# Two attention layers: TensorE's slots in pairs, sums in 32-column tiles, denominators inverted through transposes

## What is computed

```python
def layer0(x, ...):                       # x: (2, 512, 48, 48), 8 heads of 64, n = 2304 tokens
    xn = group_norm(x); qkv = qkv_w @ xn + qkv_b
    w = softmax(q . k / 8)                # per image and head: 2304 x 2304
    return proj_w @ (w . v) + proj_b + x
def layer1(h, ...):                       # queries and keys also see a position embedding
    q, k, v = [h, emb] @ Wq, [h, emb] @ Wk, h @ Wv
    return softmax(q . k / 8) . v @ Wout + bout + h
```

## Time and profile before

| | us |
|---|---|
| median of 3 runs | 4704.73 (4703.88 to 4705.93) |
| the profiled execution, its own time | 4705.96 |
| its span, first to last instruction | 4703.8 |
| granted clock of TensorE, mean | 0.993 |

### The profile page before, as it was taken

The page is one execution under the profiler, slowest core; times in us unless marked ns, Lnnn a source line. Parts: engine busy times, 40 slices in busy tenths (PEclk is TensorE's granted clock), DMA queues, the critical chain, the costliest instruction groups (busy, mean ns, idle before and its releaser), DMA issues. The chain is left out here.

```text
span 4703.8 us, 77022 instructions
## 1 busy us (share of the span) xinstructions
PE 4551.0 (97%) x25368; PEld 2453.8 (52%) x25368; DVE 3318.6 (71%) x3948; ACT 2820.0 (60%) x2981; POOL 2314.1 (49%) x1160
## 2 busy tenths in 40 slices
PE   7997999999999999998999979999999999999989
PEld 4554555555555555554555545555555555555545
DVE  4224888888888888888433358888888888888872
ACT  1113777777777777776001137777777777777750
POOL 0001666666666666666100026666666666666650
PEclk9999999999999999999999999999999999999999
DMA  4334121211111111110444431111111111111206
GB/s 192 131 124 118 25 61 28 54 35 45 42 45 45 37 45 35 48 43 32 167 146 149 147 104 31 50 38 42 46 41 45 37 47 34 50 37 45 59 20 214
DMA packets 234728, 321.66 MB, mean 68 GB/s; under 512 B 12080, under 2 KB 221104, under 8 KB 233648
## 3 DMA queue, kind: packets, MB, share of 16 engines
q1 hardware_dynamic: 214512, 292.61, 21.3%
q10 hardware_dynamic: 20160, 28.32, 1.6%
HBM read 188.76 MB, written 132.12 MB: 68 GB/s over the span
## 5 line engine op out<-in xcount | busy, mean ns | idle before, releaser
L618 POOL TENSOR_TENSOR prob<-prob,mx 128x768 f32<-128x768 f32 x1152 | 2293.1, 2025 | 2227.6 <-ACT mx L763 2227.6
L756 ACT ACTIVATE prob<-psum_att 128x1152 f32<-128x1152 f32 x1152 | 1302.3, 1130 | 587.1 <-DVE run L851 510.5
L700 PE MATMUL psum_att<-qst,kst 128*128 128x384 f32 x6912 | 1513.4, 354 | 44.6 <-DMA kst<-qk_scratch 27.4
L769 ACT ACTIVATE prob<-prob 128x1152 f32<-128x1152 f32 x1152 | 1340.8, 1164 | 356.2 <-DVE prob L618 355.2
L700 PEld LDWEIGHTS psum_att<-qst,kst 128*128 128x128 f32 x6912 | 1156.5, 189 | 452.3 <-issue 427.1
L713 PE MATMUL psum_att<-prob,vst 128*64 128x384 f32 x6912 | 1348.3, 502 | 15.4 <-ACT prob L769 9.2
L851 DVE TENSOR_TENSOR run<-psum_att,run 128x1152 f32<-128x1152 f32 x768 | 1039.1, 1353 | 370.1 <-PE psum_att L700 359.8
L618 DVE TENSOR_TENSOR prob<-prob,mx 128x384 f32<-128x384 f32 x1152 | 1015.5, 882 | 1.7 <-ACT mx L763 1.7
L713 PEld LDWEIGHTS psum_att<-prob,vst 128*64 128x64 f32 x6912 | 405.4, 136 | 532.1 <-issue 491.0
L721 PE MATMUL psum_att<-prob,const_sb 128*32 128x384 f32 x6912 | 677.1, 494 | 0.0
L321 PE MATMUL psum<-xc_l,wq 128*128 128x384 f32 x1536 | 504.1, 489 | 10.8 <-DVE hl_l L426 5.6
(11 more groups left out here) (53 smaller groups left out, 1633.6 us busy)
## 6 DMA issues: line engine op xcount, KB each, us to landing
qk_scratch<-hl_l SPq DMA_DIRECT2D x48, 1536.0 KB, 5.6
qst<-qk_scratch SPq DMA_DIRECT2D x192, 384.0 KB, 5.4
kst<-qk_scratch SPq DMA_DIRECT2D x192, 192.0 KB, 3.3
v_scratch<-vo_l SPq DMA_DIRECT2D x24, 768.0 KB, 3.5
vst<-v_scratch SPq DMA_DIRECT2D x96, 192.0 KB, 2.5
att_scratch<-ob ACTq DMA_DIRECT2D x96, 192.0 KB, 1.9
attc_l<-att_scratch SPq DMA_DIRECT2D x24, 768.0 KB, 6.0
x_sb<-in_x SPq DMA_DIRECT2D x8, 1152.0 KB, 14.3
```

The costliest lines, as they stand in the source:

```text
L618: return engine.tensor_tensor(x[:, :, q0:q1], x[:, :, q0:q1], m, ALU.subtract)
L700: mm = nc.tensor.matmul(psum[:, 3 * (s % 2) + k, 0:CH], kst[:, e, (3 * c + k) * P:(3 * c + k + 1) * P], qst[par][:, 2 * w + e, :], start=( ...
L756: nc.scalar.activation(chunk_of(par, s), s_bank(s), ACT.Copy).then_inc(copied, 1)
L769: nc.scalar.activation(x, x, ACT.Exp, scale=SCALE).then_inc(exp_done, 1)
```

## The change

TensorE's body goes by chunks: the scores of slots 2c and 2c + 1, then one `weigh` with three key tiles and one or two pairs of denominators, six times a block. The v sums are split into 32-column tiles as well, two for each head, so that all sums have one tile shape. The denominators are transposed in slot 8 (`turn_den`), added, inverted and widened by three small DVE operations on 3 x 2 numbers for each partition, transposed back in slot 10 (`spread_den`), and `norm` reads them in PSUM, in the same block, in place of block and slot t + 3, 3. The copies of both sums stand side by side at slot 6 of ACT, ahead of that slot's exp; the copy `dsp` and the six long reciprocals go. `SHIFT_DVE` stays 128 of 384.

```diff
@@ -29,17 +29,16 @@
 GN_EPS = 1e-5
 NORM_STEPS = 10
 SHIFT_DVE = 128
+POOL_BEHIND = False
 SHIFT_LAG = 15
 EXP_LAG = 16
 PV_LAG = 18
-PV_TILES = [[0, 1], [2], [3, 4], [5], [6, 7], [8], [9, 10], [11], [12, 13], [14], [15, 16, 17], []]
-DEN_PAIRS = [[], [0], [], [1, 2], [], [3], [], [4, 5], [], [6], [], [7, 8]]
-PV_END = 10
-FREE_AT = [3, 3, 7, 7, 11, 11]
-REDUCE_AT, BROADCAST_AT, SPREAD_AT = 0, 2, 8
-INVERT_AT = [9, 12, 12, 13, 13, 14]
-PARTS = len(INVERT_AT)
-NORM_AT, STORE_AT = 3, 4
+PV_COLS = 32
+DEN_PAIRS = [[0], [1, 2], [3], [4, 5], [6], [7, 8]]
+FREE_AT = [1, 1, 3, 3, 5, 5]
+TURN_AT, BROADCAST_AT = 0, 2
+EVACUATE_AT, DEN_TURN_AT, DEN_SPREAD_AT = 6, 8, 10
+STORE_AT = 0
 
 
 def is_block(t, *numbers):
@@ -648,7 +648,7 @@
                         for c in range(KC):
-                            sp.wait_ge(pv_done, pv_count(t - 2, 2 * c + 1))
+                            sp.wait_ge(pv_done, pv_count(t - 2, c))
                             sp.dma_start(
@@ -661,15 +661,17 @@
-            pe.sem_inc(pv_done, 2 * SLOTS)
+            pe.sem_inc(pv_done, 2 * KC)
...
             def bank_free(t, s):
...
-                if not before(t, 2) and s == SPREAD_AT + 2 and live(t - 2):
-                    pe.wait_ge(spread_copied, t - 1)
+                if not before(t, 2) and s == DEN_TURN_AT + 2 and live(t - 2):
+                    pe.wait_ge(den_summed, t - 1)
+                if not before(t, 3) and s == DEN_SPREAD_AT + 2 - SLOTS and live(t - 3):
+                    pe.wait_ge(normed, t - 2)
@@ -683,10 +685,16 @@
-            def spread_den(t, s):
+            def turn_den(t, s):
                 pe.wait_ge(den_copied, t + 1)
                 for r in range(3):
-                    mm = nc.tensor.matmul(spare_bank(s, r), sel, den[:, r * P:(r + 1) * P], start=True, stop=True)
+                    mm = nc.tensor.transpose(spare_bank(s, r), den[:, r * P:(r + 1) * P], ident)
+                mm.then_inc(den_turned, 1)
+
+            def spread_den(t, s):
+                pe.wait_ge(widened, t + 1)
+                for r in range(3):
+                    mm = nc.tensor.transpose(spare_bank(s, r), dwide[:, r, :], ident)
                 mm.then_inc(spread, 1)
@@ -702,17 +710,18 @@
                                               qst[par][:, 2 * w + e, :], start=(w == 0), stop=(w == 1))
                 mm.then_inc(scored, 1)
 
-            def weigh(t, par, v):
-                if v == 0 and not before(t, 1):
+            def weigh(t, par, c):
+                if c == 0 and not before(t, 1):
                     pe.wait_ge(pv_copied, t)
-                for kt in PV_TILES[v]:
-                    if kt % 3 == 0:
-                        pe.wait_ge(v_in[kt // 3], 16 * (t // JB + 1))
-                        pe.wait_ge(exp_done, SLOTS * t + 2 * (kt // 3) + 2)
+                pe.wait_ge(v_in[c], 16 * (t // JB + 1))
+                pe.wait_ge(exp_done, SLOTS * t + 2 * c + 2)
+                for kt in range(3 * c, 3 * c + 3):
                     for e in range(2):
-                        mm = nc.tensor.matmul(psum[e * D:(e + 1) * D, 6, 0:CH], vst[:, kt, e * D:(e + 1) * D],
-                                              prob[par][:, e, kt, :], start=(kt == 0), stop=(kt == KT - 1))
-                for j in DEN_PAIRS[v]:
+                        for d in range(e * D, (e + 1) * D, PV_COLS):
+                            mm = nc.tensor.matmul(psum[d:d + PV_COLS, 6, 0:CH], vst[:, kt, d:d + PV_COLS],
+                                                  prob[par][:, e, kt, :], start=(kt == 0), stop=(kt == KT - 1),
+                                                  tile_position=(0, d))
+                for j in DEN_PAIRS[c]:
                     if j == 0 and not before(t, 1):
                         pe.wait_ge(den_copied, t)
                     for e in range(2):
@@ -724,20 +733,24 @@
             def body(t, par):
-                for s in range(SLOTS):
-                    bank_free(t, s)
-                    if not before(t, 1) and live(t - 1):
-                        if s in (REDUCE_AT, REDUCE_AT + 1):
-                            turn(t - 1, s, s - REDUCE_AT)
-                        if s in (BROADCAST_AT, BROADCAST_AT + 1):
-                            broadcast_max(t - 1, s, s - BROADCAST_AT)
-                    if not before(t, 2) and live(t - 2) and s == SPREAD_AT:
-                        spread_den(t - 2, s)
-                    if live(t):
-                        scores(t, par, s)
-                    tv, pv, v = behind(t, par, s, PV_LAG)
+                for c in range(KC):
+                    for s in (2 * c, 2 * c + 1):
+                        bank_free(t, s)
+                        if not before(t, 1) and live(t - 1):
+                            if s in (TURN_AT, TURN_AT + 1):
+                                turn(t - 1, s, s - TURN_AT)
+                            if s in (BROADCAST_AT, BROADCAST_AT + 1):
+                                broadcast_max(t - 1, s, s - BROADCAST_AT)
+                        if not before(t, 2) and live(t - 2):
+                            if s == DEN_TURN_AT:
+                                turn_den(t - 2, s)
+                            if s == DEN_SPREAD_AT:
+                                spread_den(t - 2, s)
+                        if live(t):
+                            scores(t, par, s)
+                    tv, pv, sv = behind(t, par, 2 * c, PV_LAG)
                     if live(tv):
-                        weigh(tv, pv, v)
+                        weigh(tv, pv, sv // 2)
@@ -768,23 +781,13 @@
-            def copy_weighted(t, par):
-                act.wait_ge(pv_done, pv_count(t, PV_END))
-                if not before(t, 2):
-                    act.wait_ge(normed, t - 1)
-                nc.scalar.activation(pvr[par][:, :], pv_bank, ACT.Copy).then_inc(pv_copied, 1)
-
-            def copy_den(t):
-                act.wait_ge(pv_done, pv_count(t, SLOTS - 1))
+            def copy_weighted(t):
+                act.wait_ge(pv_done, pv_count(t, KC - 1))
                 if not before(t, 1):
-                    act.wait_ge(spread, t)
+                    act.wait_ge(normed, t)
+                    act.wait_ge(den_turned, t)
+                nc.scalar.activation(pvr[:, :], pv_bank, ACT.Copy).then_inc(pv_copied, 1)
                 nc.scalar.activation(den[:, :], den_bank, ACT.Copy).then_inc(den_copied, 1)
-
-            def copy_spread(t, s):
-                act.wait_ge(spread, t + 1)
-                if not before(t, 1):
-                    act.wait_ge(inverted, PARTS * t)
-                nc.scalar.activation(three(dsp[:, :]), spare(s), ACT.Copy).then_inc(spread_copied, 1)
@@ -795,19 +798,15 @@
             def body(t, par):
                 for s in range(SLOTS):
+                    if s == EVACUATE_AT and not before(t, 2) and live(t - 2):
+                        copy_weighted(t - 2)
                     te, pe_, se = behind(t, par, s, EXP_LAG)
                     if live(te):
                         exponential(te, pe_, se)
-                    if s == 5 and not before(t, 2) and live(t - 2):
-                        copy_weighted(t - 2, par)
-                    if s == 6 and not before(t, 2) and live(t - 2):
-                        copy_den(t - 2)
                     if live(t):
                         copy(t, par, s)
                     if s in (BROADCAST_AT, BROADCAST_AT + 1) and not before(t, 1) and live(t - 1):
                         copy_max(t - 1, 1 - par, s, s - BROADCAST_AT)
-                    if s == SPREAD_AT and not before(t, 2) and live(t - 2):
-                        copy_spread(t - 2, s)
                     if s == STORE_AT and not before(t, 3) and live(t - 3):
                         store(t - 3, 1 - par)
@@ -824,6 +823,8 @@
                         pool.wait_ge(copied, SLOTS * t + s + 1)
+                        if POOL_BEHIND:
+                            pool.wait_ge(dve_shifted, SLOTS * t + s + 1)
                         shift_part(nc.gpsimd, par, s, SHIFT_DVE, CH).then_inc(pool_shifted, 1)
@@ -863,36 +864,47 @@
                 dve.wait_ge(copied, SLOTS * t + s + 1)
                 shift_part(nc.vector, par, s, 0, SHIFT_DVE).then_inc(dve_shifted, 1)
 
-            def invert(t, part):
-                dve.wait_ge(spread_copied, t + 1)
+            def invert(t, s):
+                dve.wait_ge(den_turned, t + 1)
+                if live(t + 2):
+                    dve.wait_ge(scored, scored_count(SLOTS * (t + 2) + s))
                 if not before(t, 1):
-                    dve.wait_ge(normed, t)
-                q = slice(part * CH // PARTS, (part + 1) * CH // PARTS)
-                nc.vector.reciprocal(rec[:, q], dsp[:, q]).then_inc(inverted, 1)
-
-            def norm(t, par):
-                dve.wait_ge(inverted, PARTS * (t + 1))
+                    dve.wait_ge(inverted, t)
+                groups = spare(s).rearrange("p r (e o i) -> p r e o i", e=2, o=2)[:, :, :, :, 0]
```

(66 more changed lines are left out.)

## The result

The changed kernel took 4763.3 us (median of 4 runs, 4761.2 to 4763.9) against 4705.3 for the kernel before on the same chip: 1.0122 times as long, 95% interval 1.0105 to 1.014. The profiled execution's span is 4761.4 us. The forecast was 4750, range 4640 to 4840.

A forecast was written before the change was run, and what follows sets the result against it. POOL's loop through DVE's folds was to bound the changed kernel: 34.24 + 3.39 = 37.63 us, with 0.1 for the copy 37.7 a block. 92 x (37.7 - 37.17) = +49, less 4, gave 4750 us, range 4640 to 4840.

The forecast's parts named there:

- The loop through POOL: T1, POOL's second subtraction 12.23 us later, 11 subtractions, DVE's last folds, next T1: 37.63 us after the change.
- T1: TensorE's transpose of the second head's folded maximum, marking a block; forecast starts 37.4 to 38.0 us apart.
- TensorE's own work: TensorE's block after the change: 34.3 us, 2.9 less than 37.17, through fewer changes of form.
- Waits at the turns: TensorE waits for DVE's folds at both turns, 3.3 us a block, since POOL's loop ends later.
- 36.98 us, 0.19 short of the period: POOL's loop in the kernel before, 11.58 + 22.01 + 3.34 + 0.05, against a period of 37.17 us.
- T0: TensorE's transpose of the first head's folded maximum, one slot before T1; forecast to have 2 us to give.
- 0.65 + 0.1 - 0.19 = 0.56: Block's growth: POOL's loop 0.65 us longer, 0.1 for the widening copy, less 0.19 slack; forecast block 37.7 against 37.17.
- the port free at the folds: Rival: POOL done, or DVE let in twice, before DVE's folds; T1 at 35.1, 4508 us; chance near 4508: 0.06.
- The widening copy: Small DVE copy for denominators; taking its turn makes POOL's stretch 0.33 us longer; 0.1 added for that.
- The plain reading: Rival: TensorE alone bounds the kernel, its 2.9 us a block kept whole, 4434 us; chance of whole gain 0.03.

The follow-up runs named there:

- two runs: Kernel before with the subtraction shared 160 to 224, 4654.4 us; kernel before with POOL all but taken away, 4643.4 us; both 36.68 us a block.
- the kernel with the places moved: Changed kernel with subtraction shared 160 to 224, denominators' pairs dealt out anew, and their two transposes one slot earlier (slots 7 and 9): 4632.0 us.
- two of them, with POOL relieved: Kernel before with 32-column v tiles, subtraction shared 160 to 224, and three pairs of slots running their scores back to back: 4529.3 us.

## Why the prediction was right, and where not

- **The loop through POOL** was right in kind and size: second subtraction 12.23 us after T1, forecast 12.23; 11 subtractions in 22.17, forecast 22.01 and 0.1 more; POOL's end to T1 3.45, forecast 3.39. Moving the pairs out of the loop, with no less work, gave 89 us.
- **TensorE's own work**: `weigh` with two pairs 3.37, as forecast; 32-column tiles cost what 64-column ones do, and the change of form 0.14 (3.51 with wide tiles). Waits at the turns are 3.04 us, forecast 3.3.
- **"36.98 us, 0.19 short of the period" was wrong.** I closed POOL's loop only through DVE's folds to T1. It closes earlier, in slot 0. POOL's end is at 1032.99, the first head's fold ends behind it, and T0 starts at 1033.46; TensorE's undisturbed slot 0 takes 2.97 from T0 to T1, which makes 3.44. The path that ends last goes on from that fold through DVE's subtraction, ACT's exp and slot 0's v sums to T1 at 1036.58, 3.59 after POOL's end. With 11.58 and 22.01 this is 37.18, the whole period. The kernel before was bound by POOL's loop, not by TensorE, whose order takes 36.68 (two runs). The difference of period was therefore 0.65 + 0.16 - 0.13 = 0.68, where I had 0.65 + 0.1 - 0.19 = 0.56 and rounded to 0.53; the missing 0.15 us a block are 14 us, about what the forecast was low by.
- **"T1 at 35.1" for the port free at the folds**: 35.60 with POOL almost gone. The missing term is slot 5's wait for the second maximum's copy: 0.56 us, 2.86 against 2.3 for slots 4 and 5.
- **The widening copy** takes turns with POOL, 0.68 us in place of 0.36. POOL's stretch grew by 0.16 us, of which 0.12 lie in the subtraction beside the copy. I had given the copy 0.1, between nothing and a turn of 0.33; that it came out so near was luck, not a reading. In the kernel with the places moved the same copy waited a whole us longer, a term that my expectation there put at nothing.
- **The plain reading** (TensorE's 2.9 us kept whole) had no part in it. Undoing the narrow tiles cost a sixth of what it would have cost had TensorE set the end.

## What to carry to other kernels

An engine that is busy 97% of the span need not be the bound: add up every loop from one event back to itself, through each place where it can close, and compare with the period. When an engine gets faster, look where its instructions' places move within the slower loop: here a longer `weigh` between two events of POOL's loop cost more than 2.4 us less work on TensorE brought. Take the parts of such a change one by one: two of them, with POOL relieved, gave 3.8%.

## What the runs showed of the hardware

TensorE keeps its clock over the two idle pieces of the changed kernel (1.65 and 1.39 us, granted clock 1.00 in the block). With the fold as a reduction the idle time lies in one piece of 2.66 us ahead of T1. The clock then fell in 18 of some 92 blocks (0.92 to 0.96 in the mean of such a block), and their periods were 38.5 to 40.3 us in place of 37.41; in the others the same wait of about 2.66 us left it at 0.99 to 1.00. TensorE in order of time in one of the 18, and the clock (the seventh column) right behind the wait and in a usual block:

```profile
1119.09 0.90 PE L679 MATMUL psum_att<-const_sb,fold 128*128 128x128 f32 x3 [2.66 <-DVE fold L857]
1119.65 2.27 PE L708 MATMUL psum_att<-qst,kst 128*128 128x384 f32 x6
1121.85 3.78 PE L721 MATMUL psum_att<-prob,vst 128*32 128x384 f32 x24
```

```profile
1118.40:1125.20 6.80, 6.11 (x33) 3.46 (x37) 3.06 (x6) 5.55 (x6) 0.00 (x0) 0.50 0.08 29
1198.29:1235.70 37.41, 34.39 (x306) 20.28 (x307) 27.84 (x31) 27.81 (x28) 23.98 (x12) 1.00 0.11 26
```

0.50 is the lower of the two levels, 1.2 GHz. Slot 1's scores and the v sums behind them are busy 2.27 and 3.78 us there instead of 1.29 and 2.14. The Trainium skill (TensorE: Matmul & The Clock Gate, "Part 1: The HAM clock gate") tells of these two levels and of the fall after idle time; the trace agrees on the levels, and the falls here come with the wait of 2.66 us.

That the reduction took no turn beside POOL while DVE's folds and subtractions with two SBUF inputs did (2.04 against 0.56 us, 1.62 against 0.55) agrees with what the Trainium skill says of the shared ports (SBUF — State Buffer, "SBUF: two separate sides"), and so does the widening copy, 0.68 against 0.36. The reduction is a second form that does not wait, 1.49 against 1.48 us, beside the maximum with one operand in PSUM, 1.36 against 1.34.
